# Pass 2 of a graph kernel: stored units summed three at a time on three buffers

## The reference

```python
messages = _gelu(edge_input @ mW1 + mb1) @ mW2 + mb2
gates = jax.nn.sigmoid(_gelu(edge_input @ gW1 + gb1) @ gW2 + gb2)
aggregated = jax.ops.segment_sum(messages * gates, dst, num_segments=x.shape[0])
...
x = _layernorm(x + L0(x, ...))        # update MLP, residual, two layer norms
h = x @ W
msg = h[row] * norm[:, None]          # norm = dinv[row] * edge_weight * dinv[col]
out = jax.ops.segment_sum(msg, col, num_segments=N) + b
x = _layernorm(x + out)
```

## Time and profile before

| | us |
|---|---|
| median of 3 runs | 1505.38 (1504.96 to 1505.86) |
| profiled execution | 1507.1 |
| its span | 1505.3 |
| pass 1, until x1s_table is whole | about 1031 |
| POOL's gathers from x1s_table | 1031.8 to 1488.4 |
| busy in the span: PE, POOL, DVE, ACT | 1397.7, 1119.1, 1087.5, 536.7 |

### The profile page before, as it was taken

One profiled execution on the slowest core, in us unless ns is written; L12 is line 12 of the kernel. 1 busy time (PEld: TensorE's weight loads), 2 busy tenths in 40 slices (PEclk: granted clock), 3 DMA queues, 4 the chain that ended last, 5 costly groups with the idle time before them and its releaser, 6 DMA issues.

```text
span 1505.3 us, 27016 instructions
## 1 busy us (share of the span) xinstructions
PE 1397.7 (93%) x9260; PEld 1156.5 (77%) x9261; DVE 1087.5 (72%) x2883; ACT 536.7 (36%) x835; POOL 1119.1 (74%) x1192
## 2 busy tenths in 40 slices
PE   3899999999999999999999999987999999999887
PEld 2677777777777777777777677767999999998887
DVE  7688899989999988888899888867434343334234
ACT  1355555555555555555555555540000000000000
POOL 7777777777777777777777777775777777777774
PEclk9899999999999999999999999988999999999999
DMA  3455555555565556555655565557567877777772
GB/s 100 135 151 151 176 169 168 154 173 165 168 174 180 155 152 187 155 156 162 187 168 156 153 183 168 153 182 261 204 209 280 289 264 276 263 266 262 261 239 64
DMA packets 137992, 283.06 MB, mean 188 GB/s; under 512 B 53235, under 2 KB 102387, under 8 KB 137852
## 3 DMA queue, kind: packets, MB, share of 16 engines
q1 hardware_dynamic: 88860, 208.35, 38.3%
q0 software_dynamic: 37760, 58.07, 17.5%
q10 hardware_dynamic: 11232, 14.85, 3.4%
HBM read 176.08 MB, written 105.09 MB: 187 GB/s over the span
## 4 chain that ended last, share of the span: by engine, by line
PE 72%; POOL 7%; DMA 5%; DVE 4%; issue 4%; ACT 3%; DVEq 2%; SPq 0%; ACTq 0%
PE ps_hid L662 15%; PE ps_hid L685 11%; PE ps_xt L685 10%; PE ps_xt L741 10%; PE ps_win L605 9%; POOL rows L534 7%; PE ps_xt L632 5%; DMA large<-b_table 4%; PE ps_hid L659 4%; PE ps_win L823 3%; ACT large L913 3%; PE ps_bt L702 1%; DVE shared L1250 1%; PE ps_bn L716 1%; PE ps_bn L795 1%
## 5 line engine op out<-in xcount | busy, mean ns | idle before, releaser
L534 POOL DMA_INDIRECT rows<-in_x_nat,idx x782 | 741.5, 948 | 238.4 <-issue 238.0
L534 POOL DMA_INDIRECT rows<-x1s_table,idx x360 | 339.7, 944 | 118.5 <-issue 109.1
L741 PE MATMUL ps_xt<-large,x_nat 128*96 128x160 f32 (+1 forms) x2548 | 350.9, 293 | 12.8 <-DMA large<-b_table 12.8
L741 PEld LDWEIGHTS ps_xt<-large,x_nat 128*96 128x96 f32 x2548 | 333.5, 163 | 16.2 <-DMA large<-b_table 9.4
L662 PE MATMUL ps_hid<-mats,large 128*128 128x192 f32 x1568 | 321.2, 328 | 0.0
L662 PEld LDWEIGHTS ps_hid<-mats,large 128*128 128x128 f32 x1568 | 268.3, 191 | 44.2 <-issue 31.6
L913 ACT ACTIVATE large<-ps_hid 128x768 f32<-128x768 f32 x196 | 158.9, 811 | 165.2 <-PE ps_hid L662 165.2
L1250 DVE TENSOR_TENSOR shared<-cell,ps_fix 128x2000 f32<-128x2000 f32 x96 | 213.7, 2226 | 0.0
L685 PE MATMUL ps_hid<-shared 128*128 128x500 f32 x384 | 184.0, 601 | 22.5 <-ACT large L913 22.5
L685 PE MATMUL ps_xt<-shared 128*128 128x500 f32 x384 | 179.8, 591 | 6.0 <-DVE shared L1250 6.0
L953 ACT ACTIVATE shared<-ps_hid 128x1000 f32<-128x1000 f32 x96 | 96.4, 1005 | 198.3 <-PE ps_hid L685 198.3
(11 more groups left out here) (177 smaller groups left out, 1471.6 us busy)
## 6 DMA issues: line engine op xcount, KB each, us to landing
b_table<-shared SPq DMA_DIRECT2D x192, 500.0 KB
large<-b_table SPq DMA_DIRECT2D x96, 1000.0 KB, 5.2
rows<-in_x_nat,idx POOLq DMA_INDIRECT x782
large<-in_edge_t ACTq DMA_DIRECT2D x96, 128.0 KB
rows<-x1s_table,idx POOLq DMA_INDIRECT x366, 2.9
large<-in_x_t SPq DMA_DIRECT2D x7, 336.0 KB
x_nat<-in_x_nat SPq DMA_DIRECT2D x7, 336.0 KB
out_nodes<-shared SPq DMA_DIRECT2D x46, 48.0 KB
```

Source lines behind the costliest of these rows:

```text
L534: nc.gpsimd.indirect_dma_start(out=rows[slot][:, k, :], out_offset=None, in_=table, in_offset=bass.IndirectOffsetOnAxis(ap=idx[:, TG * g + ...
L741: mm = nc.tensor.matmul(raw_sums(q), x_nat[:, c, :], stored_cells(q, c), start=(c == 0), stop=(c == NB - 1))
```

## The change

Units are now summed three at a time: SIZES is (1, 2) and 15 threes, 17 turns in place of 26. All three buffers belong to one turn, so all loads of the next turn are issued after chunks 24 and 48 of this one. A turn takes three or four gathered groups (TAKES), where it took two. The ring of one-hots has a seventh place and hot_node, the placing matrices, a place of its own, both in free space of `shared`. For a turn of three, the transposes stand after 2 chunks and the placing after 5.

```diff
-PAIRS = (1, 1) + 22 * (2,) + (1, 1)
-NTURN = len(PAIRS)
+SIZES = (1, 2) + 15 * (3,)
+NTURN = len(SIZES)
...
-UNITS = [sorted(range(sum(PAIRS[0:q]), sum(PAIRS[0:q + 1])), key=lambda d: BUFFER[d % NU]) for q in range(NTURN)]
+UNITS = [sorted(range(sum(SIZES[0:q]), sum(SIZES[0:q + 1])), key=lambda d: BUFFER[d % NU]) for q in range(NTURN)]
...
-TAKES = (0, 1, 4) + 21 * (2,) + (1, 2)
-HOTS = 6
-TURN_AFTER, PLACE_AFTER, SUMS_AFTER = (5, 3), (11, 7), 32
-MAX_TURN = 6
+TAKES = (0, 1, 4, 2, 3, 4, 3, 3, 4, 3, 3, 4, 3, 3, 3, 3, 4)
+HOTS = 7
+TURN_AFTER, PLACE_AFTER, SUMS_AFTER = (5, 3, 2), (11, 7, 5), 32
+MAX_TURN = 7
...
-        sum_cols = shared[0:ND, PAST_EARLY + 3 * ND:PAST_EARLY + 3 * ND + 2 * TW]
+        sum_cols = shared[0:ND, PAST_EARLY + 3 * ND:PAST_EARLY + 3 * ND + 3 * TW]
+        NODE_AT = PAST_EARLY + 3 * ND + 3 * TW
...
-                                              for a in (dst_i[:, :].bitcast(fp32), mats, once)]
+                                              for a in (dst_i[:, :].bitcast(fp32), mats, once, shared[:, NODE_AT + 3 * W:NODE_AT + 3 * W + TG * W])]
...
-        sum_rows = spare_g[:, 0:2 * ND]
-        hot_node = spare_g[:, 2 * ND:2 * (ND + W)].rearrange("p (m w) -> p m w", m=2)
+        sum_rows = spare_g[:, 0:3 * ND]
+        hot_node = shared[0:TW, NODE_AT:NODE_AT + 3 * W].rearrange("p (m w) -> p m w", m=3)
...
-                return stored_b[:, at_b[0]:at_b[1] + 1:at_b[1] - at_b[0], h, :, j:j + WD]
+                return stored_b[:, at_b[0]:at_b[-1] + 1:at_b[1] - at_b[0], h, :, j:j + WD]
```

More of the change, by code:

```diff
@@ L92 @@
 TURNS2, PLACE, PARTS = second_pass()
-assert len(DENSE) * TG == 2 * TWOS and sum(PAIRS) == len(DENSE) and not set(EARLY) & set(DENSE)
+assert len(DENSE) * TG == 2 * TWOS and sum(SIZES) == len(DENSE) and not set(EARLY) & set(DENSE)
 assert all(b - a == 2 for a, b in zip(EARLY, EARLY[1:]))
@@ L128, in gnn_kernel @@
         PAST_EARLY = EARLY_LOW + 2 * TG * P
-        shared = sb("shared", [P, max(READY_AT + 2 * READY * CELLS, PAST_EARLY + 3 * ND + 2 * TW)])
+        shared = sb("shared", [P, max(READY_AT + 2 * READY * CELLS, PAST_EARLY + 3 * ND + 3 * TW + 3 * W + TG * W)])
         iota_i = shared[:, 2560:2560 + HW].bitcast(i32)
```

## The result

| | before | after |
|---|---|---|
| median of four runs each on one chip | 1505.62 us | 1532.75 us |
| lowest to highest | 1504.96 to 1506.16 | 1532.49 to 1535.29 |
| span of the profiled execution | 1505.3 us | 1530.4 us |
| first gather from x1s_table | 1031.81 | 1031.07 |
| last gather starts | 1487.45 | 1508.87 |

The ratio is 1.0181, 95% interval 1.0167 to 1.0194: 27 us slower. The forecast was 1526.5 us, range 1514 to 1533, so the time is inside, but only 0.25 us from its upper end.

The account below looks back on a forecast made before the run. Pass 2 was taken as bound by PE and a POOL stream delayed by every hold; holds of 18.8 us put the last gather at 1506.3, the last addition at 1513.8, plus 12.7 tail: 1526.5 us, range 1514 to 1533.

Parts of the forecast that it names:

- Which engine: Pass 2: PE and a never-resting POOL, 1.248 us a gather, both bound it; every us POOL is held ends it later.
- the bound of 1533: Whole span: upper end of the forecast, both holds with 208.5 ns a matmul, slow loads and the clock.
- 240 columns: PE's sums in turns of three: 207 ns per 240-column matmul instruction, bounds 193 and 208.5.
- PE's saving: PE's sums in pass 2: 318.1 us by threes for 324.1 before, 6 us saved if PE is the bound.
- First hold: POOL at group 9, about 1081.7 us: waits 7.7 us for turn 2's first addition; 6.3 to 7.9 by matmul price.
- Second hold: POOL at group 18: turn 5's addition waits for outputs behind three half-1 loads; 11.0 us, bounds 1.5 and 12.
- No third hold: Turn 6, also two parts: POOL wants the slot at 1211.5 plus 18.8, later than the addition at about 1222.
- PE behind POOL: Turns 9 to 15: PE waits 3 to 9 us for gathered rows, so its own speed no longer counts.
- Rival D: Half-1 loads, above all turns 3 to 5: span passes 1533 only if PE waits 2 us a turn; chance 0.06.
- The end: After the last addition: part of blocks 44 and 45 adds 4.7 and covers 1.0, tail 12.7 us for 9.0.
- Sum: Whole pass: last gather starts 1506.3, last addition ends 1513.8, plus tail 12.7 gives 1526.5, span and median alike.
- The clock: PE after its wait in turn 15: half clock could make 3 us of work take 1.6 more, upper bound only.

Follow-up runs that it names:

- half_two_y: Changed kernel with 4 of 8 gathers per group from x1s_table left out and two y buffers; 1485.49 us, ratio 0.9855 to the whole kernel before.
- half_before: Kernel before the change with 4 of 8 gathers per group from x1s_table left out (last group whole); 1491.02 us, ratio 0.9894 to that kernel whole.
- two_y: Changed kernel with a second y buffer and its own semaphore for every second part of blocks; 1527.72 us, ratio 1.0117 to the kernel before.
- outs_first: Changed kernel with the first part's outputs issued on SP ahead of the rowsum wait and three half-1 loads; 1524.60 us, ratio 1.0106 to before.
- half_after: Changed kernel with 4 of 8 gathers per group from x1s_table left out, one y buffer; 1499.17 us, ratio 0.9939 to the whole kernel before.

## Why the prediction held, and where it was off

**Which engine.** The mechanism came as forecast: two holds, a longer end, and a POOL that never catches up. That POOL never rested before, at 1.248 us a gather, and therefore pays for every us of a held slot, is what carried the forecast. POOL's last gather came 21.4 us later, the time 27. That 1532.75 still lies in the range is in part luck: the sum was 6 us short, and the bound of 1533 had been set for other reasons, a price of 208.5 ns, slow loads and the clock.

**240 columns.** 207 ns forecast, 207 measured. PE's saving was forecast as 6 us; PE was busy 7.1 us less in `half_two_y` than in `half_before`. The 5.9 us between their times match the 6 only by chance, since the longer end is in them.

**First hold.** Forecast 7.7, measured 10.4. The step was right, and three of its terms were off. POOL started at 1031.07 and not 1031.81, so its wish came 0.7 earlier. Turn 2 started 1.5 later, at 1061.58 for 1060.1. And from the end of the addition to POOL's start another 0.26 passed (1091.14 to 1091.40), which the sum left out. Turn 2 was late because turn 1 waited 1.87 us for its second unit, and then ran at the half clock for a while: the granted clock was 0.50 from 1036 to 1038 us, and the eight instructions at 1035.40 took 2.17 us, where they take 1.27 in `two_y`, whose wait of 1.27 us left the clock full. From the end of that wait to turn 2 it is 27.17 us here and 25.54 in `two_y`, 1.6 less. The sum for turn 1 counted its instructions at full clock and no load. Such a wait had to be asked about, for this turn is the first to take a unit whose load is issued last before the pass.

**Second hold.** Forecast 11.0, measured 11.8. The turn ended at 1176.5 for 1174.7. From there to the outputs' landing I had 8.2 + 2.9 = 11.1 us; y was written at 1188.06, 11.5 behind. The reading of the earlier trace rows, that small packets move only after the loads, was the hinge, and `outs_first` bears it out by moving three output DMAs. The page of the Trainium skill named in the prediction, DMA: Bandwidth & Descriptors, section Queues, rings and completion order, left room for completions out of order. In this trace SP's outputs did not pass the loads in front of them: their packets moved from about 1186 us on.

**No third hold.** Right, but by less than forecast. In turn 6 DVE waited for outputs again, 12.4 us, and turn 6's first addition ended at 1230.98, where I had about 1222. POOL took that slot at 1233.00. So the margin was 2.0 us: the second hold had moved POOL's wish just far enough.

**PE behind POOL.** I expected waits for rows of 3 to 9 us in turns 9 to 15. They were 0.6 to 5.5 us, in turns 10 to 15, 16.0 in all. The additional 8.2 us that PE waited for additions in turns 6 and 7 was not in the prediction, although each of its parts was: if y holds DVE's additions, it holds ps_win as well. By itself it costs, as the 12.6 us between `half_after` and `half_two_y` show. In the changed kernel it lay under POOL's lateness: `two_y` gained 9.6, about what POOL's gap lost.

**Loads.** Rival D gave them over 2 us a turn to matter. They cost 7.0 us in the pass, 5.8 less than before. Why less is not shown: in the halved kernels, where PE waits for no rows, it is 3.5 with two y buffers and 4.0 before, so that longer turns alone explain little of it.

**The end.** Tail 12.7 forecast, 13.4 measured. I had taken 1.0 us off, because blocks 44 and 45 would cover the wait for L796; but they wait for their own matmuls, 0.69 us at 1517.70.

**Sum.** The last gather was 2.6 us later than forecast (3.4 more of holds, for which the sum had taken 18.8 where 7.7 and 11.0 make 18.7, and 0.7 less by the earlier start), the last addition 1517.0 for 1513.8, 3.2 later; the tail adds 0.7 (the part of two blocks stands in the prediction with 4.6 and with 4.7 us; the sum took 4.7). That gives the span: 1530.4 for 1526.5. The last 2.3 us are one sentence of mine: the median of the runs is at the span. For before it was (1505.38 and 1505.3), by luck: the profiled execution of before itself took 1507.1 for its span of 1505.3. A sum made against the span needs that 1.8 to 2.1 us on top, the time of an execution around its span before and after.

**The clock.** After the waits of over 3 us the clock was again lower. PE's timeline in turn 6, and the windows view (columns after the stretch and its length: PE, PEld, DVE, ACT and POOL busy, granted clock, DMA share, GB/s):

```profile
1195.33 4.77 PE L824 MATMUL ps_win<-hot,rows 128*96 128x72 f32 x32 [4.61 <-DVE acc L1445]
1199.89 2.77 PE L824 MATMUL ps_win<-prod,rows 128*96 128x72 f32 x16
...
1206.29 9.65 PE L742 MATMUL ps_xt<-large,x_nat 128*96 128x240 f32 x38
...
1197.00:1199.00 2.00, 2.00 (x15) 2.00 (x15) 1.85 (x4) 0.00 (x0) 1.69 (x2) 0.50 1.02 424
...
1207.00:1209.00 2.00, 2.00 (x6) 1.41 (x5) 1.41 (x8) 0.00 (x0) 1.68 (x2) 0.50 0.26 51
```

0.50 is 1.2 GHz for 2.4. At full clock 16 instructions of L824 take 1.5 us (at 1075.34) and 32 at most 3.0, six of L796 0.88 (at 1168.57), and the 38 take 8.02. Here they took 4.77, 2.77, twice 1.55 and 9.65: about 6 us lost in turn 6, more than the wait of 4.61 that came before. I had priced one such stretch at 1.6. Short waits cost something in places too. In turn 14 PE waited 1.35 us:

```profile
1446.99 1.58 PE L824 MATMUL ps_win<-hot,rows 128*96 128x72 f32 x16 [1.35 <-DMA rows<-x1s_table,idx]
1448.40 1.34 PE L796 MATMUL ps_bn<-w_gcn,acc 96*128 96x96 f32 x6
1449.53 9.22 PE L742 MATMUL ps_xt<-large,x_nat 128*96 128x240 f32 x38
```

The granted clock was 0.50 from 1450 to 1452, and 1.7 us were lost. After 1.54 us in turn 13 the same rows took 0.85 and 8.01.

All this stayed off the end, because the rows of turn 15 landed when POOL had them ready, whatever PE had lost before. The Trainium skill, TensorE: Matmul & The Clock Gate, section HAM oscillation, has the direction, half-speed work after waits between bursts; the amount here is from the rows.

## What to carry to other kernels

When an engine runs without a gap through a whole pass, every buffer that it takes has a due time; write those down before making the turns of its consumer longer, for here a saving on the consumer was worth nothing while the releases came later. Small outputs that free a buffer belong ahead of large loads in the same queue, or need a second buffer: here either was worth about 10 us. Small batches belong where the producer has no slack, and at the end, where the whole last batch stands behind the last data; bigger ones did no harm in the second half of the pass, and whether they gained anything there was too small to tell.

## What was not expected of the hardware

Moving three output DMAs of 48 KB ahead of three loads of 1 MB brought the time from issue to where DVE could write y from 10.1 us (1177.92 to 1188.06) to 5.4 at most (1172.82 to 1178.25, with no wait seen), on the same queue. In the changed kernel the gathers of the other queue moved 0.20 MB beside those loads, while the outputs behind them waited. And the half clock after a wait of 4.61 us cost more than the wait had: about 6 us over the next 20. The length of a wait alone did not say what it would cost: after 1.46 us before 1346.99, 1.54 in turn 13 and 1.27 in `two_y` PE went on at full clock, after 1.87 us in turn 1 and 1.35 in turn 14 it lost about 1.6 and 1.7 us.
